# An adaptive layer norm transformer layer on one core: a weight-sum block, two modulation pieces and the order of the first heads moved

## The reference

```python
x = L0_attn_x                                    # (4, 512, 512)
mod = (_silu(L0_c) @ L0_wmod).reshape(4, 6, 1, -1)
sa, ca, ga, sb, cb, gb = (mod[:, k] for k in range(6))
ga = (2 * (ga >= 0) - 1) * jnp.maximum(jnp.abs(ga), 0.25)
gb = (2 * (gb >= 0) - 1) * jnp.maximum(jnp.abs(gb), 0.25)
h = _layernorm(x, axis=-1) * (1 + ca) + sa
x = x + ga * attention(h)                        # 16 heads of 128, causal
h = _layernorm(x, axis=-1) * (1 + cb) + sb
x = x + gb * ffn(h)                              # 8 experts top-2, one shared MLP
```

## Time and profile before

| what | value |
|---|---|
| median of 3 runs | 1550.49 us (1550.35 to 1550.74) |
| the profiled execution's own time | 1549.2 us |
| span of its trace | 1547.2 us |
| PE busy | 1511.7 us (98%) |
| DVE, ACT, POOL busy | 993.6, 735.6, 718.3 us |
| mean granted TensorE clock | 0.996 of full |

### The profile page before, as it was taken

The page is one execution under the profiler, slowest core; times in us unless marked ns, Lnnn a source line. Parts: engine busy times, 40 slices in busy tenths (PEclk is TensorE's granted clock), DMA queues, the critical chain, the costliest instruction groups (busy, mean ns, idle before and its releaser), DMA issues.

```text
span 1547.2 us, 29330 instructions
## 1 busy us (share of the span) xinstructions
PE 1511.7 (98%) x8844; PEld 1346.9 (87%) x8844; DVE 993.6 (64%) x2222; ACT 735.6 (48%) x1743; POOL 718.3 (46%) x763
## 2 busy tenths in 40 slices
PE   7799999998999999999999999999999999999998
PEld 3688778887999999999999999988999999999997
DVE  5877676667777777777777777784458322222268
ACT  3442222345666666666666666663332233333333
POOL 1313333345756566656566665669822311111054
PEclk9999999999999999999999999999999999999999
DMA  8234655569767666675747485636243555765566
GB/s 296 100 126 170 215 187 193 201 237 311 231 178 230 185 208 189 202 213 166 235 141 251 144 252 181 209 131 238 70 175 143 184 198 188 279 228 203 186 193 196
DMA packets 203295, 304.05 MB, mean 197 GB/s; under 512 B 80384, under 2 KB 142208, under 8 KB 196048
## 3 DMA queue, kind: packets, MB, share of 16 engines
q1 hardware_dynamic: 196096, 281.80, 53.7%
q0 software_dynamic: 5680, 18.62, 4.1%
q10 hardware_dynamic: 1440, 2.62, 0.5%
HBM read 187.35 MB, written 115.64 MB: 196 GB/s over the span
## 4 chain that ended last, share of the span: by engine, by line
PE 87%; POOL 4%; DVE 4%; issue 2%; DMA 2%; ACT 1%; SPq 0%; ACTq 0%; POOLq 0%; DVEq 0%
PE bank L1566 46%; PE bank L1666 17%; PE bank L1781 7%; PE bank L1733 7%; PE bank L1764 4%; PE bank L1831 2%; PE bank L1867 1%; PE bank L1580 1%; POOL acc L1015 1%; POOL acc L1013 1%; DMA ffn_rows<-h 1%; POOL h L1028 1%; POOL h L1030 1%; DMA xin<-ffn_rows 0%; DVE h L2615 0%
## 5 line engine op out<-in xcount | busy, mean ns | idle before, releaser
L1566 PE MATMUL bank<-w,xt_hi 128*128 (+2 forms) x1136 | 281.7, 330 | 0.3 <-ACT gate_s L1492 0.2
L1566 PEld LDWEIGHTS bank<-w,xt_hi 128*128 128x128 f32 x1136 | 196.9, 189 | 6.9 <-DVE xt_lo L2195 0.6
L1566 PE MATMUL bank<-w,xt_lo 128*128 (+2 forms) x568 | 183.9, 324 | 0.0
L1390 ACT ACTIVATE prob<-prob,row_inv 128x128 f32<-128x128 f32 (+3 forms) x256 | 137.3, 560 | 79.3 <-DVE row_inv L2232 79.1
L2349 DVE TENSOR_TENSOR ht_lo<-bank,ht_hi 128x128 fp32r<-128x128 f32 (+1 forms) x213 | 48.4, 282 | 179.8 <-ACT ht_hi L1507 179.7
L1378 ACT ACTIVATE prob<-bank,neg_max 128x128 f32<-128x128 f32 (+3 forms) x256 | 133.8, 526 | 42.1 <-DVE neg_max L2224 41.9
L1566 PE MATMUL bank<-wv_hi,h_hi 128*128 128x256 f32 x512 | 147.0, 287 | 0.0
L1566 PE MATMUL bank<-wv_hi,h_lo 128*128 128x256 f32 x512 | 144.7, 283 | 0.0
L1566 PE MATMUL bank<-wv_lo,h_hi 128*128 128x256 f32 x512 | 144.7, 283 | 0.0
L1566 PE MATMUL bank<-w,ht_hi 128*128 (+3 forms) x426 | 139.2, 408 | 4.4 <-DVE ht_lo L2349 4.3
L1191 POOL DMA_INDIRECT xin<-ffn_rows,slot_tokens x39 | 39.8, 1021 | 185.6 <-PE bank L1831 181.2
(11 more groups left out here) (248 smaller groups left out, 4137.7 us busy)
## 6 DMA issues: line engine op xcount, KB each, us to landing
keys<-k_ring SPq DMA_DIRECT2D x64, 512.0 KB, 3.0
ch_raw<-wexp SPq DMA_DIRECT2D x128, 170.0 KB, 3.2
experts_hi<-ch_hi SPq DMA_DIRECT2D x128, 170.0 KB, 2.6
experts_lo<-ch_lo SPq DMA_DIRECT2D x128, 170.0 KB, 2.7
w<-experts_hi SPq DMA_DIRECT2D x10, 2176.0 KB, 7.9
w<-experts_lo SPq DMA_DIRECT2D x10, 2176.0 KB, 14.3
q_transposed<-q_out SPq DMA_DIRECT2D x64, 256.0 KB, 2.0
k_even<-keys SPq DMA_DIRECT2D x16, 1024.0 KB, 5.5
```

Of the source, the lines that this page charges most:

```text
L1390: ins = act.activation(part, part, ACT.Copy, scale=row_inv[:, h, r:r + 1])
L1566: ins = pe.matmul(dst, a, m, start=(k == 0), stop=(k == last))
```

## The change

- POOL: sums(0) comes ahead of seed(2).
- ACT: `batch(1)` comes behind the second evicted head, not the third; within a batch the second high part comes ahead of the last hidden tile.
- DVE: t_low(0) is done in the order 2, 3, 1, normalise(2), 4; in half(0) hidden(2, 2) and the low parts of h of batch 2 come earlier. PE follows: products 3 and 4 of half(0) ahead of the transposes of batch 2, and the banks of plain(2) in another order.
- Piece 5 is made behind half(0) on PE, into bank 7, and copied by ACT to `mod_raw5`; DVE finishes piece 2 behind half(2) and piece 5 behind half(3). Piece 4 is made in the first attention step, between turn(0) and turn(1), and finished by one DVE instruction. weigh(1) waits for that.
- `bias_rows(3)` goes from ACT to POOL's list in the first step, behind a wait for all four mod stores, the last of which SP issues at the end of its first step.
- At the start of stage 3 `load_xin(1)` is issued ahead of `load_shared(1)`.

```diff
-MOD_AFTER = {4: 2, 8: 4, 12: 5}
-MOD_ORDER = [0, 1, 3, 2, 4, 5]
+MOD_AFTER = {2: 2, 3: 5}
+MOD_ORDER = [0, 1, 3, 2, 5, 4]
+MOD_EV = {0: 1, 1: 2, 3: 3, "raw5": 4, 2: 5, 5: 6, 4: 7}
-PLAIN_BANKS = [[0, 1, 2, 3], [0, 1, 2, 3], [7, 0, 1, 2], [3, 6, 7, 0]]
+PLAIN_BANKS = [[0, 1, 2, 3], [0, 1, 2, 3], [0, 1, 2, 7], [3, 6, 7, 0]]
...
             raw_weights(1)
+            sp.wait_ge(mod_full, 4)
+            mod_weights(5, w_x)
...
+                if v == 4:
+                    sp.wait_ge(mod_ev, MOD_EV[5])
+                    mod_weights(4, w_x)
...
                 for q in range(2, count):
                     chunk(q)
+                if first:
+                    store_mod(4)
...
                     load_shared(0, WG, WU)
                     store_h2(0, 1, 2)
-                    load_shared(1, WU, WD)
                     sp.wait_ge(h2_st, 32)
                     load_xin(1)
+                    load_shared(1, WU, WD)
                     load_shared(2, WD, WE)
...
             seed(1)
+            sums(0)
             seed(2)
-            sums(0)
             sums(1)
...
                     bias_rows(2)
+                    pool.wait_ge(mod_st, 4 * 16)
+                    bias_rows(3)
...
             def batch(b):
                 hidden(b, 1)
                 high(b, 0)
+                high(b, 1)
                 hidden(b, 3)
-                for i in range(1, TT):
-                    high(b, i)
+                high(b, 2)
+                high(b, 3)
...
-                    if b == 0 and j == 2:
+                    if b == 0 and j == 1:
                         batch(1)
...
                 if v == 0:
                     batch(2)
+                    act.wait_ge(mod_full, MOD_ORDER.index(5) + 1)
+                    act.activation(mod_raw5, bank[7][0:B, :], ACT.Copy).then_inc(mod_ev, 1)
...
                 if v == NV - 2:
-                    act.wait_ge(mod_full, 6)
-                    bias_rows(3)
...
                 product(1, sum_w(1), t_rows(2))
+                t_ready(2)
+                product(2, sum_w(2), t_rows(3))
+                t_ready(4 if s else 3)
+                product(3, sum_w(0), t_rows(1))
+                product(4, plain_w(2, 0), rows(2))
                 if v == 0:
                     transposes(2, 0)
                     transposes(2, 1)
-                t_ready(2)
-                product(2, sum_w(2), t_rows(3))
-                t_ready(4)
-                product(3, sum_w(0), t_rows(1))
+                product(5, sum_w(3), rows(DC + 2))
                 if v == 0:
                     transposes(2, 2)
                     transposes(2, 3)
-                product(4, plain_w(2, 0), rows(2))
-                product(5, sum_w(3), rows(DC + 2))
+                t_ready(4)
                 product(6, plain_w(2, 1), t_rows(4))
-                if v in MOD_AFTER and MOD_AFTER[v] != 2:
-                    pe.wait_ge(*reader(v, 4))
-                    mod_piece(MOD_AFTER[v], w_x, half_banks(v + 1)[5])
+                if v == 0:
+                    mod_piece(5, w_x, 7)
...
                 turn(0)
-                if not first:
+                if first:
+                    mod_piece(4, w_x, 7)
+                else:
                     values(2)
                     values(3)
                 turn(1)
...
+                if first:
+                    pe.wait_ge(mod_ev, MOD_EV[4])
                 weigh(1)
...
-            t_low(0, (2, 3, 4))
-            normalise(2)
...
                 if v in PREPARE:
                     unit_low(PREPARE[v])
+                if v == 0:
+                    hidden(2, 2)
...
                 if v == 0:
-                    hidden(2, 2)
+                    for j in range(TT):
+                        h_low(2, j)
...
+                if b == 1:
+                    t_low(0, (2, 3, 1))
+                    normalise(2)
+                    t_low(0, (4,))
...
+                if first:
+                    dve.wait_ge(mod_full, MOD_ORDER.index(4) + 1)
+                    dve.tensor_scalar(mod_row[4], bank[7][0:B, :], 1.0, None, ALU.add).then_inc(mod_ev, 1)
```

More of the change, by code:

```diff
@@ L601, in stage1_over @@
             eng.wait_ge(k22_ok, NK)
-            eng.wait_ge(mod_ev, 6)
+            eng.wait_ge(mod_ev, MOD_EV[5])
         def reader(v, k):
@@ L700, in half @@
                             first_loads()
+                if v in MOD_AFTER:
+                    store_mod(MOD_AFTER[v])
                 if v == 3:
@@ L803, in step @@
                         load_chunk(q)
+                if tail == 0:
+                    sp.wait_ge(mod_st, 4 * 16)
                 if tail >= 0:
@@ L850, in step @@
                     load_xin(3)
-            sp.wait_ge(mod_st, 4 * 16)
             walk_steps(sp, step)
@@ L1570, in _ @@
             pe.wait_ge(silu_c, 1)
-            MOD_FREE = {3: (mod_ev, 1), 2: (modc_ok, 2), 4: (mod_ev, 4), 5: (mod_ev, 5)}
+            MOD_FREE = {3: (mod_ev, 1), 2: (modc_ok, 2), 5: reader(0, 1), 4: (s_exp, 3)}
             def mod_piece(m, w, to):
-                pe.wait_ge(modw_ld[m], {4: 32, 5: 48}.get(m, 16))
+                pe.wait_ge(modw_ld[m], {5: 32, 4: 48}.get(m, 16))
                 if m in MOD_FREE:
@@ L1609, in _ @@
             PLAIN_FREE = [[None] * 4, [(q_ev, j + 1) for j in range(4)],
-                          [reader(0, 1), reader(0, 2), reader(0, 3), reader(0, 4)],
-                          [reader(0, 5), reader(0, 6), (q_ev, 9), (q_ev, 10)]]
+                          [reader(0, 2), reader(0, 3), reader(0, 4), (mod_ev, MOD_EV["raw5"])],
+                          [reader(0, 5), reader(0, 6), (q_ev, 12), (q_ev, 9)]]
             def plain(b):
@@ L1641, in half @@
                         free.append(reader(m // 7 + 1, m % 7) if m >= 0 else
-                                    [(q_ev, 11), (q_ev, 12), None, None, (q_ev, 13), (q_ev, 14), (q_ev, 15), (q_ev, 16)][m])
-                if v - 1 in MOD_AFTER and MOD_AFTER[v - 1] != 2:
-                    free[5] = (mod_ev, MOD_ORDER.index(MOD_AFTER[v - 1]) + 1)
+                                    [(q_ev, 10), (q_ev, 11), None, None, (q_ev, 13), (q_ev, 14), (q_ev, 15), (q_ev, 16)][m])
                 at = 2 * s * DC
@@ L2157, in half @@
                 total(d12, p3, ba, u_s)
-                if v == 0:
-                    for j in range(TT):
-                        h_low(2, j)
                 free(2)
@@ L2165, in half @@
                     m = MOD_AFTER[v]
-                    mod_piece(m, mod_raw if m == 2 else bank[half_banks(v + 1)[5]][0:B, :])
+                    mod_piece(m, mod_raw if m == 2 else mod_raw5)
                 if v == 0:
@@ L2183, in plain @@
                     t_low(1, (2, 3, 4))
-                if b % 2:
-                    t_low(b // 2, (1,))
+                if b == 1:
+                    t_low(0, (2, 3, 1))
+                    normalise(2)
+                    t_low(0, (4,))
+                if b == 3:
+                    t_low(1, (1,))
             stage1_order(plain, half)
```

36 lines of the change are left out of this document (14 added, 22 removed).

## The result

| | median | range | executions |
|---|---|---|---|
| before | 1550.42 us | 1550.03 to 1550.74 | 4 |
| changed | 1535.76 us | 1535.61 to 1537.87 | 4 |

The ratio is 0.9911, with a 95% interval of 0.9899 to 0.9923: 14.7 us faster between the medians. The profiled execution of the changed kernel is the longest of its four, 1537.87 us with a span of 1535.7 us, so its trace explains 11.5 us (1547.2 − 1535.7). The profiled execution before was 1.3 us under its median, the one after is 2.1 above: 3.4 of the 14.7 us lie between executions and are in no trace.

What follows compares the result with a forecast made beforehand. PE, busy 98% of the span, bounds the kernel. Gains of 6.0 (stage 1 chain), 7.2 (pieces), 1.3 (clock) and 0 sum to 14.5 us: 1549.2 to 1534.7 profiled, 1536.0 as median; forecast range 1533.5 to 1538, chance 0.56.

Steps and rivals of the forecast that it cites:

- (a): Stage 1: batch(1) moved earlier on ACT shrinks two PE waits, so plain(1) starts 2.7 us sooner.
- (b): Stage 1: POOL's early weight sums run beside DVE's newton steps and normalise(1); loss 1.0 us, bounds 0 and 2.2.
- (c): Stage 1: DVE's chain from t_sums(0) to stats(3) loses three waits, 3.0 us, and disturbance, 1.3; gain 4.3 us.
- (d): Modulation pieces 4 and 5 move from gapless PE stretches into waits at turn(1) and plain(2); gain 7.2 us.
- (e): First attention step: with the gap filled, PE's clock should not fall; gain 1.3 us, bounds 0 and 1.7.
- (f): Stage 3 start: xin(1) comes 1.4 us earlier but later loads shift; net nothing, bounds −1.5 and +2.5.
- (g): First attention step: bias_rows(3) on POOL, 2.28 us of copies plus a store wait, stays hidden with 2 us to spare.
- 0.05 us to spare: First attention step: piece 4's 3.60 us fit into PE's 3.65 us wait ahead of turn(1).
- R1: Rival: ports take 1.2 us more and the clock falls behind batch 3's transposes; gain 11.7, 1538.8 us; chance 0.17.
- a tail that moves by more than 1.5 either way: Stage 3 to the end: a shift of the tail beyond 1.5 us would show the prediction wrong.

Runs made afterwards that it cites:

- run 5: The changed kernel run again without any edit, beside the kernel before on the same chip: 1535.3 us, ratio 0.9906.
- run 3: Changed kernel with ACT's batch(1) back behind the third head and the old order within a batch: 1540.93 us, ratio 0.9926.
- run 4: Changed kernel with POOL's early sums(0) made to wait until DVE has normalised batch 1: 1537.89 us, ratio 0.9906.
- run 2: Changed kernel with sums(0) back behind seed(2) on POOL: 1542.64 us, ratio 0.9933.
- run 6: Changed kernel with modulation piece 5's product made twice behind half(0): 1537.59 us, ratio 0.9918.
- run 9: Changed kernel with modulation piece 4 made from one of its four chunks: 1537.68 us, ratio 0.9925.
- run 8: Changed kernel with row tile 1's store and load on ACT's queue, sums(0) behind normalise(1), fourth modulation store ahead of chunk stores: 1533.47 us; repeat 1534.53 us.
- the three mends: Edits to the changed kernel: row tile 1's store and load on ACT's queue, sums(0) behind normalise(1), fourth modulation store ahead of chunk stores: 1533.47 us.
- the early store: Row tile 1's store issued on SP ahead of the first shared weights, added to the three mends: repeat 1533.04 us, ratio 0.9897.
- run 7: Changed kernel with row tile 1's store and load back on ACT's queue, beside SP's weight pieces, at stage 3's start: 1534.52 us, ratio 0.9899.
- run 10: Run 8's kernel (run 8) with row tile 1's store on SP ahead of the shared weights: four executions 1532.3 to 1533.75 us; repeat 1533.04 us.
- Run 1: Changed kernel with load_xin(1) put back behind the second weight piece, load_shared(1): 1537.43 us, ratio 0.9901.

## Why the prediction was right, term by term

The time (1536.0 foretold, 1535.76 measured) and the sum (14.5 foretold, 14.7 between the medians) agree, closer than the working deserves. The main terms came as reckoned, but the losses were larger, and the traces explain 11.5 us (13.1 in run 5), not 14.5. The prediction reckoned from a profiled execution 1.3 us under the median, to 1534.7 us for the new one; the profiled execution took 1537.87. That the medians agree to 0.2 us is partly luck. The terms, read at their own places:

| term | foretold | measured | from |
|---|---|---|---|
| (a) batch 1 earlier | 2.7 | 2.63 | run 3 |
| (b) sums beside the newton steps | −1.0 | −1.34 | run 4 |
| (c) DVE chain | 4.3 | 4.4 to 4.7 | 5.69 − 2.63 + 1.34; run 2: 3.40 + 1.34 |
| (d) two modulation pieces | 7.2 | 7.5 | 13.23 − 5.69 |
| (e) clock, first attention step | 1.3 | 1.0 | 14.25 − 13.23 |
| (f) tail | 0 | −2.8 by tile 3, −1.5 five tiles on | the two traces |
| (g) bias_rows(3) | 0, 2 us to spare | −0.4, nothing to spare | 13.81 − 14.25 |

(a) was costed from two waits: the first went, the second shrank to 0.75 where 0.5 was foretold. plain(1) started at 40.79, which looks like the 40.5 to 41 foretold; with the start taken off it is 41.41, a gain of 1.2 for (a) and (b) together where 1.7 was foretold.

(b) lay within its bounds. Three steps were caught, each for the rest of a sum; the fourth was not, and the larger tiles lost 0.29 in 1.92. Large operations are slowed and not shut out, as in the earlier trace rows: beside sums(1), 51 to 56 us, two instructions of t_low took 2.90 together and a third 1.72 where one alone takes 1.22, and POOL's sums stretched from 0.74 to between 1.59 and 1.71. The Trainium skill (SBUF — State Buffer, "SBUF: two separate sides") says that the shared pair of ports is locked for a whole instruction and that the other engine fully blocks. This case's traces agree for the small steps, 0.61 to 0.67 beside sums of 0.73, and not for t_low, which lost 0.23 to 0.50 each beside sums that take 0.74 alone.

(c) The three waits went, and t_sums kept 1.22 each. Run 2 shows that two of them, 2.4 of the 3.0 us, hung on the sums. The new order of t_low, hidden and h_low was reckoned at nothing in this chain; no run undoes it, so a part of the 4.4 may be its own.

(d) No wait stood before or behind piece 5. Run 6 shows that the chain on DVE is the later one by some 1.7 us, and run 9 that piece 4's place costs nothing. The "0.05 us to spare" were enough. The 0.3 above 7.2 are not explained.

(e) The clock did stay at 1.00, and 1.0 of the 1.3 came. The only new wait up to there is 0.23 us for DVE's finishing of piece 4 at weigh(1), which the prediction put at some 0.2; the 0.55 behind DVE was there before.

(f) is where the working failed. The steps were right: the tile earlier by 1.4 (1.86 against 3.25), a loss at the up half (0.95), a loss at xin(2) (1.98). What was missing was their sum, 4.79 against 3.25, and that the clock may fall behind the third; R1 had such a fall, but in stage 1, behind the wait at the transposes of batch 3 (1.66 us), where it didn't come. The prediction named a tail that moves by more than 1.5 either way as a sign of being wrong, and by tile 3 it moved by 2.8. Later tiles gave back 1.2, most of it the wait of 1.12 at 1103.04, so that 1.5 remained. The parts of the gain were understood, the price of the moved load was not.

(g) The store landed at 384.8, 12 us sooner than the 397 foretold in the time of before (the new time is 14 earlier there, so 2 late). The slack of 2 us was gone, with a price of 0.4, and with the store moved ahead in run 8 the price is gone too.

The errors of size, 0.3 in (e), 0.4 in (g) and 1.5 to 2.8 in (f), would have made the sum 11 to 12; the profiled trace says 11.5 and run 5's 13.1, the spans of the other executions 13.6 to 13.8. Run 5, whose tail to tile 3 is as long, differs behind tile 3: 477.3 us from there to the end against 479.1 in the first trace, which lists waits of 0.8 us for a gathered row tile and of 0.6 that run 5 doesn't have. What brings these on in one execution and not in another stays open.

## What to carry to other kernels

Work that must be done somewhere is free in a gap whose end another engine sets; check it by adding the same work again (here piece 5) or by taking it away (here piece 4). When a load is moved ahead of others in one queue, add up the waits of everything behind it: here a gain of 1.4 us was bought with 2.9. Keep GpSimd's work from running beside a chain of tiny VectorE instructions; here three of them lost about half a microsecond each, and starting the sums 2.9 us later cost nothing. Compare with the times of the same stretch in other traces before a difference of 1 us is believed. The best version tried puts the three mends and the early store together: 1533.0 us, 2.3 to 2.7 below the changed kernel from different groups, 1.4 to 2.2 by the ratios to the kernel before, whose intervals overlap.

## What the runs showed of the chip that was not expected

- A gap's length alone doesn't tell whether the clock falls to its lower level. It didn't after 3.25 us in the kernel before nor after 1.86 at 1036; it did after 1.98 at 1048, the third of three gaps within 14 us, and at once after 2.65 to 3.57 us at row tile 1 in runs 7, 8 and 10 (0.83 to 0.89 from 1030 to 1040). Run 1 has the order of the kernel before and a wait of 3.36 at the same place, and there it fell (0.93, then 0.89). In run 9 three gaps of 1.86, 1.60 and 2.53 us at the start of stage 3 left it at 1.00.
- A store of 256 KB took 6.2 us on ACT's queue behind 3.8 MB issued on SP's in the 3.2 us before it, and 2.9 on SP's queue ahead of the weights; its load back, on ACT's queue both times, took 4.5 and 7.4. Here the second queue gave no precedence.
- One execution took 5773.5 us, with PE busy for 5758.8 us, 3.8 times the changed kernel's 1507.5 (the largest groups of matmuls took 2.3 to 3.6 times as long each, the products of the experts 856 ns in place of 330), DVE's busy time hardly changed (1012.4 us), and a granted clock recorded as 1.00. It is left out of all comparisons, and its cause is open.
